# GpSimd's slot-list writes of the attention stage, issued one to a turn

## The chip, the cores and the metric

The kernel runs on one core of a Trainium2 chip. The metric is the device time of one execution in microseconds, the median of several runs.

## What is computed

A layer of self-attention (16 sequences of 256 tokens, 256 features, 16 heads) with a residual and a layer norm is followed by a mixture of 8 experts (two per token, capacity 1280 slots each) with a residual and a layer norm. Cut to what matters here:

```python
gates = softmax(x_flat @ gating_w)                 # x_flat: 4096 tokens after attention and layer norm
topk_w, topk_idx = top_k(gates, 2)
norm_w = topk_w / (sum(topk_w) + 1e-08)
onehot = (flat_e[:, None] == arange(8)[None, :])
position = cumsum(onehot, axis=0) - 1              # the slot of a token's pair in its expert's buffer
valid = position < capacity
buf = zeros((8, capacity, d)).at[flat_e, pos_scatter].set(x_flat[flat_t], mode='drop')
h = maximum(einsum('ecd,edh->ech', buf, w1) + b1, 0)
out_e = einsum('ech,ehd->ecd', h, w2) + b2
out = zeros_like(x_flat).at[flat_t].add(out_e[flat_e, pos] * w_eff)
```

## The kernel before

The attention stage runs over turns, eight to a sequence. Every engine walks the same turns in its own program, and a table of offsets says in which turn a step of sequence m stands: a step with offset 40 of sequence 3 stands in turn 8*3+40. The turns are only an order in which each engine's instructions are written out. No engine waits for a turn; it waits for semaphores alone. So two steps of one engine trade places only if another step stands in a turn between the old and the new one.

For each sequence GpSimd (POOL) does four things in the order of its turns. It splits the transposed x into a high and a low part (L543, L547). It turns the row statistics `mv` into `rstd` and `shift` of the layer norm (L554 to L560), which wait for VectorE's `mv_done`. For the sequences 0 to 11 it works out the slots `dest` and the token and weight `item` (function `entries`, L486 to L524); for the sequences 12 to 15 VectorE does that (`last_entries`, ending in `weight_done` at L869). Then it writes these entries to the slot list in HBM with four indirect DMAs (L533, function `into_lists`): two tiles of 128 tokens, c, and two choices of expert, k. Each DMA writes 128 entries of 8 bytes. `dest` and `item` have four buffers, so sequence m uses number m % 4.

The constant WRITE holds the turns of the writes, one tuple for each step, and in each tuple an offset for the ordinary sequences (0 to 11), one for the sequences 12 and 13, one for 14 and one for 15. The writes of sequence 13 (`FIRST`) are issued in turn 153 instead, after the layer-norm factors of sequence 14.

What hangs on the writes stands at the end of the attention stage. SyncE's queue (SP) loads the list of expert 0 for the first 256 slots as soon as all writes of the sequences 0 to 11 have landed (`list0_loaded`), the next 256 slots when those of sequence 12 have landed too (`list1_loaded`), and behind that the early part of the other experts' lists (L443). GpSimd then gathers the rows of these two chunks with two indirect DMAs each (L1348, `gather(0, 0)` and `gather(0, 1)`, turn 149), and TensorE transposes the gathered rows (L1664). After the writes of the sequences 13, 14 and 15 the late part of the lists is loaded (L454, L455), and the expert stage goes on with the later chunks.

Of the kernel before, what the change touches and what calls it, by code (L numbers as in the profile page):

```python
# [41 lines left out]
def build(nc, x_d, wq_d, wk_d, wv_d, wo_d, gw_d, w1_d, b1_d, w2_d, b2_d, out_d):  # L42
# [40 lines left out]
    with top:  # L83
# [21 lines left out]

        g = locals()
        first = attention(nc, g)
        second = experts(nc, g)
        g["lists"] = second[9]
# [32 lines left out]
def due(turn, offset, count):  # L142


    n, rest = divmod(turn - offset, 8)
    return n if rest == 0 and 0 <= n < count else None
# [11 lines left out]
def pair_of(turn, offset, count):  # L158


    n, u = divmod(turn - offset, 8)
    return (n, u) if 0 <= n < count else None


def attention(nc, g):
    (x_v, x1_v, acc_v, list_v, x1_d, acc_d, list_d) = (
        g["x_v"], g["x1_v"], g["acc_v"], g["list_v"], g["x1_d"], g["acc_d"], g["list_d"])
    NB, S, D, T, R, H = g["NB"], g["S"], g["D"], g["T"], g["R"], g["H"]
    QC, DK, HH, NE, FT, FF, CAP, BLK = g["QC"], g["DK"], g["HH"], g["NE"], g["FT"], g["FF"], g["CAP"], g["BLK"]
    SCALE, TRASH, TOPK = g["SCALE"], g["TRASH"], g["TOPK"]  # L170
# [8 lines left out]
    with ctx:  # L179
        def sem(name):  # L180
            return ctx.enter_context(nc.semaphore(name))

        def sb(name, shape, dt=F32):
            return ctx.enter_context(nc.sbuf_tensor(name, shape, dt))
# [74 lines left out]
        dest = [sb(f"dest{i}", [P, QC, TOPK], I32) for i in range(4)]  # L259
        item = [sb(f"item{i}", [P, QC, TOPK, 2], I32) for i in range(4)]  # L260
# [36 lines left out]
        listed = [sem(f"listed{i}") for i in range(4)]  # L297
# [5 lines left out]
        UT, AT, O, LIST = 34, 36, 38, 50  # L303
        LN, LG, PICK, SEEN, EX = (40, 40, 40, 40), (41, 41, 41, 41), (43, 43, 43, 42), (44, 43, 43, 42), (45, 44, 45, 43)
        X1, STORE, POS, SLOT = (42, 46, 45, 44), (48, 48, 48, 45), (46, 44, 45, 43), (47, 45, 45, 44)
        ENTRY, WRITE = (48, 45, 45, 44), ((51, 46, 46, 45), (52, 47, 50, 46))
        LAST = 8 * (NB - 1) + WRITE[1][3] + 1
        LTAIL = NB - 4
        EARLY, FIRST = g["EARLY"], NB - LATE
        END = 8 * (NB - 1)  # L310
# [13 lines left out]
        def routed(turn, stage):  # L324

            for m in range(NB):
                if turn == 8 * m + stage[0 if m < LTAIL else max(m - NB + 4, 1)]:
                    return m
            return None
# [41 lines left out]
        def sync_program(sp, lists):  # L371
# [14 lines left out]

            for turn in range(LAST + 1):
                n = due(turn, -14, NB)
# [68 lines left out]
        def gpsimd_program(pool, gather):  # L457
# [65 lines left out]
                pool.wait_ge(token_done, m + 1)  # L523
                nc.gpsimd.tensor_scalar(tok[:, :], tok[:, :], float(S), None, ALU.add).then_inc(tok_done, 1)  # L524

            def into_lists(m, c):
                if m == 0 and c == 0:
                    pool.wait_ge(filled, 80)
                pool.wait_ge(dest_done, m + 1)
                pool.wait_ge(token_done, m + 1)  # L530
                pool.wait_ge(weight_done, m + 1)
                for k in range(TOPK):
                    nc.gpsimd.indirect_dma_start(  # L533
                        out=list_d, out_offset=bass.IndirectOffsetOnAxis(ap=dest[m % 4][:, c, k:k + 1], axis=0),
                        in_=item[m % 4][:, c, k, :], in_offset=None, bounds_check=NE * CAP - 1,
                        oob_is_err=False).then_inc(listed[m % 4], 16)

            for turn in range(LAST + 1):
                n = due(turn, XT, NB)
                if n is not None and n >= 2:  # L540
                    pool.wait_ge(xT_copied, n - 1)
                    pool.wait_ge(v_ready, QC * (n - 1))
                    nc.gpsimd.tensor_copy(xT_hi[n % 2][:, :, :], xT_f[:, :, :]).then_inc(xT_hi_done, 1)  # L543
                n = due(turn, XT + 1, NB)
                if n is not None and n >= 2:
                    pool.wait_ge(xT_hi_done, n + 1)
                    nc.gpsimd.tensor_tensor(xT_lo[n % 2][:, :, :], xT_f[:, :, :], xT_hi[n % 2][:, :, :].bitcast(F32),  # L547
                                            ALU.subtract).then_inc(xT_lo_done, 1)
                m = due(turn, LN[0] + 1, NB)
                if m is not None:  # L550
                    pool.wait_ge(mv_done, m + 1)
                    pool.wait_ge(x1_done, m)
                    pool.wait_ge(ex_done, QC * m)
                    nc.gpsimd.tensor_scalar(veps[:, :], mv[:, :, 1], EPS, None, ALU.add).then_inc(norm_parts, 1)  # L554
                    pool.wait_ge(norm_parts, 2 * m + 1)
                    nc.gpsimd.tensor_tensor(rstd[:, :], veps[:, :], expo[:, 0:QC], ALU.pow).then_inc(rstd_done, 1)
                    nc.gpsimd.tensor_scalar(nmean[:, :], mv[:, :, 0], -1.0, None, ALU.mult).then_inc(norm_parts, 1)
                    pool.wait_ge(norm_parts, 2 * m + 2)
                    pool.wait_ge(rstd_done, m + 1)
                    nc.gpsimd.tensor_tensor(shift[:, :], nmean[:, :], rstd[:, :], ALU.mult).then_inc(shift_done, 1)  # L560
                m = due(turn, LIST, LTAIL)
                if m is not None:
                    entries(m)
                for c in range(QC):
                    m = routed(turn, WRITE[c])
                    if m is not None and m != FIRST:
                        into_lists(m, c)
                    if turn == END - 8 + LN[0] + 1:
                        into_lists(FIRST, c)
                if turn == END + PV0 + 4:  # L570
                    pool.wait_ge(v_ready, QC * NB)
                    pool.wait_ge(g["list0_loaded"], 16)
                    gather(0, 0)
                    pool.wait_ge(g["list1_loaded"], 16)
                    gather(0, 1)

        def scalar_program(act, rows_hi, relu):
# [39 lines left out]

            for turn in range(LAST + 1):
                if turn == K + 2:
# [86 lines left out]
        def vector_program(dve, rows_lo, halves):  # L706
# [166 lines left out]

            for turn in range(LAST + 1):
                if turn == K + 2:
# [95 lines left out]
        def tensor_program(pe, transposes, layer1):  # L971
# [95 lines left out]

            for turn in range(LAST + 1):
                p = pair_of(turn, S0, NB)
# [119 lines left out]
            pe.wait_ge(y_done, QC * NB)  # L1189

        return sync_program, gpsimd_program, scalar_program, vector_program, tensor_program


# [602 lines left out]
```

## Time and profile before

| | |
|---|---|
| median of 3 runs | 822.04 us (821.6 to 822.65) |
| span of the profiled execution | 856.8 us |
| TensorE busy | 784.5 us, 92% |
| VectorE busy | 605.1 us, 71% |
| ScalarE busy | 442.1 us, 52% |
| GpSimd busy | 410.2 us, 48% |
| GpSimd slot-list writes (L533) | 64 DMAs, 65.5 us |

The profile shows one execution, and gives its span but no time of its own beside it; the span is 34.8 us longer than the median of the runs. Rows of the timeline give the start and the length of a group of instructions in us, the engine, the line, the operation and its tiles, and in brackets how long the engine sat idle before and what ended that. The turns of the attention stage end at about 380 us; the experts follow.

### The profile page before, as it was taken

The numbers are of one execution on the slowest core, as the hardware profiler recorded it, in microseconds if no ns is written. First come the engines' busy times: TensorE is split into PE (matmuls) and PEld (weight loads), VectorE is DVE, ScalarE is ACT, GpSimd is POOL, SyncE is SP. The second block draws the span as 40 slices with busy tenths as digits, with TensorE's granted clock in tenths as the row PEclk, the third lists the DMA queues.
The fourth block names the chain that finished last, engine by engine and source line by source line (L and its number), as shares of the span: only waits on it lengthen the run. The fifth ranks groups of instructions, "written<-read, shape, count | busy, mean of one in ns | idle before, by whom it ended". The sixth has DMA issues, their size and how long they took to land.

```text
span 856.8 us, 16628 instructions
## 1 busy us (share of the span) xinstructions
PE 784.5 (92%) x5919; PEld 648.5 (76%) x5919; DVE 605.1 (71%) x1325; ACT 442.1 (52%) x753; POOL 410.2 (48%) x595
## 2 busy tenths in 40 slices
PE   7699989999989985896999999999999999999994
PEld 7577766677667653585889898898898888988993
DVE  5768878888888885683756856756657568665983
ACT  3166757777666664542534534534345345443670
POOL 1011245555555546457146445254364462556675
PEclk9799999999999998799899999999999999999998
DMA  5677765555555572326145245253352451533741
GB/s 158 135 165 161 161 153 113 114 113 114 116 114 110 115 141 73 116 51 180 20 91 109 41 89 115 43 130 50 81 111 40 96 112 31 140 57 57 288 179 46
DMA packets 71534, 92.75 MB, mean 108 GB/s; under 512 B 12972, under 2 KB 55885, under 8 KB 71324
## 3 DMA queue, kind: packets, MB, share of 16 engines
q1 hardware_dynamic: 53308, 67.95, 31.0%
q0 software_dynamic: 16928, 22.15, 14.9%
q10 hardware_dynamic: 1216, 1.57, 0.8%
q8 instruction: 48, 0.79, 0.4%
q14 instruction: 34, 0.28, 0.1%
HBM read 39.18 MB, written 26.89 MB: 77 GB/s over the span
## 4 chain that ended last, share of the span: by engine, by line
PE 69%; DVE 14%; issue 5%; POOL 3%; another core or an unknown queue 3%; DMA 2%; ACT 2%; ACTq 1%; POOLq 0%; DVEq 0%; SPq 0%
PE bank L1718 14%; DVE negm L890 10%; PE wide L1687 8%; PE wide L1685 8%; PE wide L1686 8%; PE bank L985 7%; PE bank L1720 7%; PE wide L1030 5%; PE bank L1664 2%; PE wide L1048 2%; PE bank L1095 2%; PE bank L1064 1%; PE bank L994 1%; POOL slot_list L533 1%
## 5 line engine op out<-in xcount | busy, mean ns | idle before, releaser
L1359 POOL DMA_INDIRECT acc_rows<-o_w,lists x70 | 120.4, 1720 | 181.6 <-ACT o_w L1508 167.9
L890 DVE TENSOR_REDUCE negm<-wide 128x4 f32<-128x1024 f32 x128 | 156.1, 1222 | 50.5 <-PE wide L1030 31.7
L630 ACT ACTIVATE probs<-wide 128x1024 f32<-128x1024 f32 x128 | 131.0, 1024 | 89.1 <-PE wide L1048 68.9
L1475 ACT ACTIVATE h<-wide,b1T 128x512 f32<-128x512 f32 (+1 forms) x200 | 115.0, 600 | 96.8 <-PE wide L1687 69.1
L1720 PE MATMUL bank<-stack,h_lo 128*128 128x256 f32 x560 | 156.9, 280 | 0.0
L1685 PE MATMUL wide<-g_hi,stack 128*128 128x512 f32 (+1 forms) x400 | 140.8, 352 | 5.2 <-DVE g_lo L1536 4.1
L1687 PE MATMUL wide<-g_hi,stack 128*128 128x512 f32 (+1 forms) x400 | 140.1, 350 | 0.1
L1686 PE MATMUL wide<-g_lo,stack 128*128 128x512 f32 (+1 forms) x400 | 140.1, 350 | 0.0
L1508 ACT ACTIVATE o_w<-o_b,lists 128x256 f32<-128x256 f32 x70 | 35.7, 510 | 148.6 <-DVE o_b L1646 135.5
L1718 PE MATMUL bank<-stack,h_hi 128*128 128x512 f32 x304 | 108.7, 401 | 1.3 <-DVE o_b L1646 1.3
L1720 PEld LDWEIGHTS bank<-stack,h_lo 128*128 128x128 f32 x560 | 105.6, 189 | 0.0
L1348 POOL DMA_INDIRECT rows<-x_rows,lists x80 | 84.3, 1054 | 29.5 <-issue 23.9
L1718 PE MATMUL bank<-stack 128*128 128x512 f32 x256 | 90.4, 396 | 0.0
L1685 PEld LDWEIGHTS wide<-g_hi,stack 128*128 128x128 f32 x400 | 75.9, 190 | 16.4 <-DVE g_lo L1536 4.4
L1030 PE MATMUL wide<-stack 48*128 48x256 f32 x512 | 65.5, 335 | 24.8 <-DVE negm L890 21.2
L1030 PEld LDWEIGHTS wide<-stack 48*128 48x128 f32 x512 | 40.2, 191 | 62.0 <-DVE negm L890 28.7
L1644 DVE TENSOR_TENSOR low<-bank,b_all 128x256 f32<-128x256 f32 x70 | 29.6, 422 | 81.4 <-PE bank L1720 69.4
L1687 PEld LDWEIGHTS wide<-g_hi,stack 128*128 128x128 f32 x400 | 75.9, 190 | 10.6 <-issue 0.3
L1686 PEld LDWEIGHTS wide<-g_lo,stack 128*128 128x128 f32 x400 | 76.0, 190 | 9.7
L1064 PE MATMUL bank<-probs,v_aug 128*32 128x256 f32 x1024 | 72.4, 402 | 9.3 <-ACT probs L630 9.3
L543 POOL CAST xT_hi<-xT_f 128x512 fp32r<-128x512 f32 x14 | 8.5, 610 | 148.3 <-ACT xT_f L585 148.3
L533 POOL DMA_INDIRECT slot_list<-item,dest x64 | 65.5, 1023 | 25.7 <-issue 23.6
(211 smaller groups left out, 1640.9 us busy)
## 6 DMA issues: line engine op xcount, KB each, us to landing
stack<-qk SPq DMA_DIRECT2D x180, 128.0 KB, 4.2
w_raw<-in_L_ffn_w SPq DMA_DIRECT2D x16, 1024.0 KB
x_sb<-in_L_attn_x SPq DMA_DIRECT2D x16, 256.0 KB, 5.1
x_rows<-x SPq DMA_DIRECT2D x16, 256.0 KB
acc_rows<-x SPq DMA_DIRECT2D x16, 256.0 KB
acc_sb<-acc_rows SPq DMA_DIRECT2D x8, 512.0 KB, 11.1
out<-acc_sb SPq DMA_DIRECT2D x8, 512.0 KB
x_rows<-zrow SPq DMA_DIRECT2D x2, 1152.0 KB, 6.6
```

The source lines that it names most:

```text
L630: nc.scalar.activation(probs[:, i % 4].rearrange("p x c t -> p x (c t)"), shifted_banks(i)[:, :, :], ACT.Exp, scale=SCALE).then_inc(exp_do ...
L890: nc.vector.tensor_reduce(negm[n % 2][:, :, :, u].rearrange("p c x -> p x c"), score_banks(PAIRS * n + u)[:, :, :].rearrange("p x (c t) -> ...
L1030: ins = nc.tensor.matmul(out[:, x, c * S:c * S + S], st[k, u, 0, c * P:c * P + P], st[k, u, 1, :], start=True, stop=True, tile_position=(H ...
L1064: ins = nc.tensor.matmul(out, v_aug[n % VB][:, c, 4 * t + j, :], probs[:, u % 4, j % 2, c, :], start=(c == 0), stop=(c == QC - 1), tile_po ...
L1348: nc.gpsimd.indirect_dma_start(out=rows[c][:, r, :], out_offset=None, in_=x1_d, in_offset=bass.IndirectOffsetOnAxis(ap=lists[:, e, QC * c ...
L1359: nc.gpsimd.indirect_dma_start(out=acc_d, out_offset=bass.IndirectOffsetOnAxis(ap=lists[:, e, QC * c + r, 0:1], axis=0), in_=o_w[c][:, r, ...
L1475: ins = nc.scalar.activation(h[u % 2][:, t], banks[BZ[u % 4]][:, t], ACT.Relu, bias=b1T[:, FT * e + f:FT * e + f + 1])
L1685: nc.tensor.matmul(out, w1_hi[:, k, fs], g_hi[i % 2][:, k, cols], start=(k == 0), stop=False)
L1686: nc.tensor.matmul(out, w1_hi[:, k, fs], g_lo[i % 2][:, k, cols], start=False, stop=False)
L1687: ins = nc.tensor.matmul(out, w1_lo[:, k, fs], g_hi[i % 2][:, k, cols], start=False, stop=(k == DK - 1))
L1718: nc.tensor.matmul(banks[BO[r]], H_hi[:, f, rs], w2_both[:, f, :, :].rearrange("p x d -> p (x d)"), start=(f == 0), stop=False)
L1720: ins = nc.tensor.matmul(out_half(r, 1), H_lo[:, f, rs], w2_hi[:, f, :], start=False, stop=(f == FT - 1))
```

## The change

The table of the writes gets four entries instead of two, one for each DMA, and `into_lists` issues one DMA instead of two. Each call carries the three waits that formerly stood ahead of a pair.

```diff
-        ENTRY, WRITE = (48, 45, 45, 44), ((51, 46, 46, 45), (52, 47, 50, 46))
-        LAST = 8 * (NB - 1) + WRITE[1][3] + 1
+        ENTRY, WRITE = (48, 45, 45, 44), ((52, 46, 46, 45), (53, 47, 46, 45), (54, 48, 50, 46), (55, 49, 50, 46))
+        LAST = 8 * (NB - 1) + WRITE[3][3] + 1
...
-            def into_lists(m, c):
-                if m == 0 and c == 0:
+            def into_lists(m, i):
+                c, k = divmod(i, TOPK)
+                if m == 0 and i == 0:
                     pool.wait_ge(filled, 80)
                 pool.wait_ge(dest_done, m + 1)
                 pool.wait_ge(token_done, m + 1)
                 pool.wait_ge(weight_done, m + 1)
-                for k in range(TOPK):
-                    nc.gpsimd.indirect_dma_start(
-                        out=list_d, out_offset=bass.IndirectOffsetOnAxis(ap=dest[m % 4][:, c, k:k + 1], axis=0),
-                        in_=item[m % 4][:, c, k, :], in_offset=None, bounds_check=NE * CAP - 1,
-                        oob_is_err=False).then_inc(listed[m % 4], 16)
+                nc.gpsimd.indirect_dma_start(
+                    out=list_d, out_offset=bass.IndirectOffsetOnAxis(ap=dest[m % 4][:, c, k:k + 1], axis=0),
+                    in_=item[m % 4][:, c, k, :], in_offset=None, bounds_check=NE * CAP - 1,
+                    oob_is_err=False).then_inc(listed[m % 4], 16)
...
-                for c in range(QC):
-                    m = routed(turn, WRITE[c])
+                for i in range(QC * TOPK):
+                    m = routed(turn, WRITE[i])
                     if m is not None and m != FIRST:
-                        into_lists(m, c)
+                        into_lists(m, i)
                     if turn == END - 8 + LN[0] + 1:
-                        into_lists(FIRST, c)
+                        into_lists(FIRST, i)
```

The four other engines' instructions stand exactly as before. On GpSimd the place of most writes is an ordinary sequence, here the second one: its last step on `tok`, the four writes, and the x split of a later sequence. Before:

```order
L524 TENSOR_SCALAR tok<-tok 128x2 [waits token_done]
L533 DMA slot_list<-item,dest 10240x2 [waits weight_done,token_done,dest_done]
L533 DMA slot_list<-item,dest 10240x2
L533 DMA slot_list<-item,dest 10240x2 [waits weight_done,token_done,dest_done]
L533 DMA slot_list<-item,dest 10240x2
L543 CAST xT_hi<-xT_f 128x512 [waits v_ready,xT_copied]
L547 TENSOR_TENSOR xT_lo<-xT_f,xT_hi 128x512 [waits xT_hi_done]
```

After:

```order
L524 TENSOR_SCALAR tok<-tok 128x2 [waits token_done]
L533 DMA slot_list<-item,dest 10240x2 [waits weight_done,token_done,dest_done] x4
L543 CAST xT_hi<-xT_f 128x512 [waits v_ready,xT_copied]
L547 TENSOR_TENSOR xT_lo<-xT_f,xT_hi 128x512 [waits xT_hi_done]
L554 TENSOR_SCALAR veps<-mv 128x2 [waits ex_done,x1_done,mv_done]
```

No instruction traded places there; the second and the fourth write carry three waits of their own now. The same holds for the writes of the sequences 13, 14 and 15.

The one place where GpSimd's order differs is the end of the attention stage, from the last `tok` of sequence 11 to the first gathers. `item3,dest3` are sequence 11, `item0,dest0` sequence 12, and L554 to L560 are the layer-norm factors of sequence 13. Before:

```order
L524 TENSOR_SCALAR tok<-tok 128x2
L533 DMA slot_list<-item3,dest3 10240x2 x4
L533 DMA slot_list<-item0,dest0 10240x2 x4
L554 TENSOR_SCALAR veps<-mv 128x2
L556 TENSOR_TENSOR rstd<-veps,expo 128x2
L557 TENSOR_SCALAR nmean<-mv 128x2
L560 TENSOR_TENSOR shift<-nmean,rstd 128x2
L1348 DMA rows0<-x1_rows,lists 128x256 x2
L1348 DMA rows1<-x1_rows,lists 128x256 x2
```

After:

```order
L533 DMA slot_list<-item3,dest3 10240x2 x2
L533 DMA slot_list<-item0,dest0 10240x2
L533 DMA slot_list<-item3,dest3 10240x2
L533 DMA slot_list<-item0,dest0 10240x2
L533 DMA slot_list<-item3,dest3 10240x2
L533 DMA slot_list<-item0,dest0 10240x2
L554 TENSOR_SCALAR veps<-mv 128x2
L556 TENSOR_TENSOR rstd<-veps,expo 128x2
L557 TENSOR_SCALAR nmean<-mv 128x2
L560 TENSOR_TENSOR shift<-nmean,rstd 128x2
L533 DMA slot_list<-item0,dest0 10240x2
L1348 DMA rows0<-x1_rows,lists 128x256 x2
```

The writes of the two sequences alternate from the third on, and the last write of sequence 12 moved behind the four small steps of the layer norm of sequence 13, just ahead of the gathers.

## Rows read from the trace of the kernel before

**Rows 1.** The page: the span, and TensorE's granted clock in 40 slices.

```profile
span 856.8 us, 16628 instructions
...
PEclk9799999999999998799899999999999999999998
```

**Rows 2.** Timeline of POOL, writes of an ordinary sequence and what follows them.

```profile
252.78 0.98 POOL L533 DMA_INDIRECT slot_list<-item,dest  x1 [0.30 <-issue]
254.07 0.97 POOL L533 DMA_INDIRECT slot_list<-item,dest  x1 [0.30 <-issue]
255.34 0.97 POOL L533 DMA_INDIRECT slot_list<-item,dest  x1 [0.30 <-issue]
263.06 0.61 POOL L543 CAST xT_hi<-xT_f 128x512 fp32r<-128x512 f32 x1 [6.75 <-ACT xT_f L585]
```

**Rows 3.** Timeline of POOL, the end of the attention stage.

```profile
328.88 0.97 POOL L533 DMA_INDIRECT slot_list<-item,dest  x1 [0.30 <-issue]
...
332.70 0.97 POOL L533 DMA_INDIRECT slot_list<-item,dest  x1 [0.30 <-issue]
...
336.53 0.97 POOL L533 DMA_INDIRECT slot_list<-item,dest  x1 [0.30 <-issue]
341.33 0.22 POOL L554 TENSOR_SCALAR veps<-mv 128x2 f32<-128x2 f32 x1 [3.83 <-DVE mv L939]
...
344.87 1.20 POOL L560 TENSOR_TENSOR shift<-nmean,rstd 128x2 f32<-128x2 f32 x1
346.23 1.10 POOL L1348 DMA_INDIRECT rows<-x_rows,lists  x1 [0.17 <-issue]
...
348.88 0.95 POOL L1348 DMA_INDIRECT rows<-x_rows,lists  x1 [0.30 <-issue]
350.13 0.95 POOL L1348 DMA_INDIRECT rows<-x_rows,lists  x1 [0.30 <-issue]
```

**Rows 4.** Timeline of DVE, one stop in a sequence, and around the last writes.

```profile
257.51 1.23 DVE L890 TENSOR_REDUCE negm<-wide 128x4 f32<-128x1024 f32 x1 [1.34 <-remote]
...
331.60 0.17 DVE L869 TENSOR_TENSOR item<-ex,inv_t 128x4 f32<-128x4 f32 x1
...
342.21 0.67 DVE L956 CAST stack<-w_raw 128x1024 fp32r<-128x1024 f32 x1
...
344.78 1.23 DVE L958 TENSOR_TENSOR stack<-w_raw,stack 128x1024 fp32r<-128x1024 f32 x1
```

**Rows 5.** Timeline of SP's DMA queue, the list loads and what follows.

```profile
342.46 2.02 SPq L440 DMA_DIRECT2D lists<-slot_list  x2
344.53 0.43 SPq L443 DMA_DIRECT2D lists<-slot_list  x1
358.22 0.37 SPq L406 DMA_DIRECT2D x_rows<-x  x1
```

**Rows 6.** DMA issues, KB each and median us from issue to landing.

```profile
lists<-slot_list SPq DMA_DIRECT2D x2, 2.0 KB, 1.7
```

**Rows 7.** The chain that ended last: start, us, and what.

```profile
329.99 9.16 another core or an unknown queue
...
359.81 0.23 POOL veps L554
...
380.63 3.17 DMA slot_list<-item,dest
```

**Rows 8.** Timeline of PE, the transposes of the first gathered rows.

```profile
360.85 0.60 PE L1664 MATMUL bank<-ident,rows 128*128 128x128 f32 x4
...
364.99 0.63 PE L1664 MATMUL bank<-ident,rows 128*128 128x128 f32 x4
```

**Rows 9.** Timeline of POOL, behind the layer norm of sequence 14.

```profile
361.24 0.20 POOL L560 TENSOR_TENSOR shift<-nmean,rstd 128x2 f32<-128x2 f32 x1
...
368.13 0.97 POOL L533 DMA_INDIRECT slot_list<-item,dest  x1 [1.12 <-issue]
...
376.96 1.89 POOL L533 DMA_INDIRECT slot_list<-item,dest  x1 [0.30 <-issue]
```

## The prediction

> **What bounds the kernel now.** I read the page first for the span [rows 1], then the chain of work that ended last. The chain is mostly TensorE, but from 359.81 us to the landing of a list write that starts at 380.63 it goes through GpSimd's queue [rows 7]: there GpSimd's instructions are on the path that sets the end, and a microsecond lost on them is lost in the time. Next I read GpSimd's timeline in three places: an ordinary sequence, where the writes are far from any limit; the end of the attention stage, where the change reorders them; and the stretch on the chain, where it only adds waits. Last, SP's queue and TensorE's transposes say who waits for the reordered writes.
>
> In an ordinary sequence the last write ends at 255.34 + 0.97 = 256.31, and GpSimd then sits idle for 6.75 us until ScalarE's copy of the transposed x is there [rows 2]. Nothing on GpSimd waits behind the writes, and nobody reads the list before the end of the stage.
>
> **The change part by part.** *The turns of the sequences 0 to 10.* Moving the four writes from the turns 51 and 52 to 52 to 55 passes no other GpSimd instruction: the printed order is the same, and an engine doesn't wait for turns. So the writes will stand where they stood, back to back, one each 1.27 us. Cost 0 us. If the idle 6.75 us behind them were gone, a longer run of writes would push the x split of a later sequence; nothing here makes the run longer, though.
>
> *The waits.* 32 of the 64 writes get three waits more, all for semaphores that the write ahead of them has seen already. The rows show both kinds before the change: the write at 254.07 has three waits in front of it, those at 252.78 and 255.34 have none, and all three come 0.30 us behind their predecessor [rows 2]. So a set of satisfied waits between two writes costs 0. A bound from above: GpSimd's 1.12 us in front of the write at 368.13 [rows 9], less the plain 0.30, is 0.82 us, but that one really waited for VectorE. On the chain six writes get such waits (two each of the sequences 13, 14, 15), so the bound is 6 x 0.82 = 4.9 us; I take 0, since the rows at 0.30 are the same case and that one isn't. A gain is excluded, as nothing is taken away.
>
> *The alternation of sequences 11 and 12.* The third write is now the first of sequence 12. It needs VectorE's weights, which are there at 331.60 + 0.17 = 331.77 [rows 4], while GpSimd has finished the second write at 328.88 + 0.97 = 329.85 and would be ready at 330.15 [rows 3]. In the order before, sequence 12 began at 332.70 and waited for nothing. So GpSimd now stands for about 1.7 us and issues its third to seventh write from about 331.9 on, 1.27 us apart; the seventh ends at 331.9 + 4 x 1.27 + 0.97 = 338.0. Before, the eighth ended at 336.53 + 0.97 = 337.50. Behind it stand the layer-norm factors of sequence 13, and they waited for VectorE's `mv` until 341.33, after 3.83 us of idleness [rows 3]. The hole is covered by these 3.83 us; without that cover it would cost 0.5 us. Cost 0.
>
> *The last write of sequence 12.* It now follows the shift of sequence 13, which ends at 344.87 + 1.20 = 346.07 [rows 3]. With a gap of some 0.6 us (an estimate between the 0.30 and the 1.12 of the rows) it starts at about 346.7 and ends at 347.7. The first gather slips from 346.23 to about 348.0. SP may load the second list piece only when this write has landed: 346.7 + 3.17 = 349.9, with the landing time of the write on the chain [rows 7]. It was issued between 342.46 and 344.48 before [rows 5]. It lands 1.7 us later [rows 6], at 351.6, and so the gathers of the second chunk start at about 351.9 instead of 348.88 and end 2.2 us later, at 354.1. Who waits? GpSimd's own next step is the layer norm of sequence 14, at 359.81 [rows 7]: 5.7 us of cover. SP's queue holds the early list of the other experts behind it, which is read only after all attention work, and then the store at 358.22 [rows 5]; SP is free at about 350.8. TensorE transposes the first chunk at 360.85 and the second at 364.99 [rows 8]; with some 2 to 3 us for a gather to land (estimate from the 3.17 and the 1.7 above), the rows are there by about 353 and 357. Cover 8 us each. Cost 0; beyond 5.7 us of further delay it would count on the chain one for one.
>
> The Trainium skill ("SBUF — State Buffer", section "SBUF: two separate sides") has a rule that speaks against the new place: GpSimd can't write the descriptors of its DMAs while VectorE runs a copy that uses both ports. VectorE splits w1 from 342.21 to 346.01 [rows 4], and GpSimd's shift took 1.20 us in that stretch against 0.20 us later [rows 3, 9]; the trace agrees that GpSimd suffers there. By the rows the moved write starts after 346.07, clear of it; by the rule, if it fell into it, it would take something like the 1.89 us of the write at 376.96 [rows 9] instead of 0.97, 0.9 us more, also under the cover. The sum would be 0 by either.
>
> **The sum** is 0 + 0 + 0 + 0. It is made on the profiled execution (span 856.8 us), and I carry differences to the median of 822.04 us one to one. The 34.8 us between them matter for the risk, since the trace holds stops that no semaphore explains. One of 9.16 us, with an unnamed releaser, stands just in the stretch of the reordered writes [rows 7].
>
> **The rivals.** *Slower: the cover is made by that stop.* If the timed executions don't have the 9.16 us, the layer norm of sequence 14 is due at 350.65. TensorE's clock is 0.7 of full on average in slice 16, 342.7 to 364.1 us [rows 1], after the stop; had it stayed high, the 17.1 us from 342.7 to 359.8 could be 12.0, and the step due at 345.5. GpSimd then runs without idling: factors of sequence 13 from 338.1 to 339.7 (1.63 us, as 359.81 to 361.44 [rows 7, 9]), the moved write at 340.3, landing at 343.5, the list at 345.2, the second gathers over at 347.7. They would keep the layer norm of sequence 14 waiting 2.2 us; 0.8 us of that is given back where GpSimd waits for VectorE's entries of sequence 14 anyway (1.12 against 0.30 [rows 9]). That is +1.4 us, 823.4. The order before has its second gathers over at about 344, so pays nothing. It passes 0.2% (1.64 us, about what a measurement of this kernel tells from no change) when that step is due before 345.2, and reaches +2.8 us at 343.6. For it: the gap of 34.8 us. Against it: I can't see which of these stops a timed run has, and every step must shrink by the full amount.
>
> *Faster: the unbroken run of writes is itself what stops the others.* ScalarE resumes at 329.99 + 9.16 = 339.15, 1.65 us after the eighth write has ended; in the ordinary sequence VectorE resumes at 257.51 after a stop of 1.34 us, 1.20 us after the fourth write [rows 2, 4]. If eight unbroken writes make 9.16 us and four make 1.34, a run broken by the 1.7 us hole into two and five would make about 3.3 us by interpolation: up to 5.9 us less in the trace, a time near 816 to 821, say 819. Against it: no engine but GpSimd waits for the issue of a write.
>
> *The change does something in ordinary sequences after all*, by its waits: bound +4.9 us above, and any value of 0.27 us a write or more on the chain would pass 0.2%. Nothing but that one far row speaks for it.
>
> **How the numbers follow.** No effect beyond 0.5 us: 0.60. The covered gathers become visible: 0.24, somewhat more than half of it above 0.2%. A shorter stop: 0.11. The waits cost something, or code fetched at other moments: 0.05, mostly small or up. So faster 0.12, same 0.66, slower 0.22. The time is that of the first case, with a trifle for the runs' own spread: 822.2 us; its own range is 821.4 to 823.2. The range for 8 in 10 reaches into the slower rival to +2.6 us (824.6) and into the faster one to -1.4 us (820.6).
>
> **What would show it.** In the changed kernel's timeline of GpSimd: four writes of an ordinary sequence still 1.27 us apart with 0.30 us between all of them, and the idle time behind them near 6.7 us; a hole of about 1.7 us before the third of the last run; the moved write near 346.7, a list load by SP near 350, the second gathers near 352, and the layer norm of sequence 14 still ended by VectorE's `mv`, near 359.8. The forecast is wrong if that last step is ended by a gather instead, if the gap between writes grows, or if the stop of 9.16 us changes its length.

## The result, and the profile after

The change made the kernel slower. Its median is 824.72 us in six runs (823.86 to 826.41) against 821.82 us for the kernel before in six runs beside it; the ratio is 1.0047, with a 95% interval of 1.0037 to 1.0058, which is 3.0 to 4.8 us, 3.9 us in the middle. The ratios in this document are not quotients of two medians; these two medians alone lie 2.9 us apart. The forecast was 822.2 us with a range up to 824.6.

The page of the changed kernel has a span of 822.6 us, 34.2 us less than the one that the prediction was read from, and TensorE's clock doesn't dip in the slices of the stretch:

```profile
span 822.6 us, 16660 instructions
...
PEclk9689999999999999999999999999999999999998
...
PE 77%; DVE 13%; issue 4%; POOL 3%; DMA 2%; ACTq 1%; ACT 0%; POOLq 0%; DVEq 0%; SPq 0%
```

The stops with unnamed releasers are gone from it, too. So the two pages can't be laid side by side, and I took a second profile of the kernel before (the first experiment below). This is GpSimd's timeline there, with a span of 817.7 us, at the place that answers to [rows 3]:

```profile
308.88 1.12 POOL L533 DMA_INDIRECT slot_list<-item,dest  x1 [0.55 <-issue]
310.30 0.98 POOL L533 DMA_INDIRECT slot_list<-item,dest  x1 [0.30 <-issue]
...
315.00 0.97 POOL L533 DMA_INDIRECT slot_list<-item,dest  x1 [1.17 <-DVE item L869]
...
318.91 0.97 POOL L533 DMA_INDIRECT slot_list<-item,dest  x1 [0.30 <-issue]
319.95 1.02 POOL L554 TENSOR_SCALAR veps<-mv 128x2 f32<-128x2 f32 x1
322.20 0.23 POOL L560 TENSOR_TENSOR shift<-nmean,rstd 128x2 f32<-128x2 f32 x1
...
325.59 0.95 POOL L1348 DMA_INDIRECT rows<-x_rows,lists  x1 [0.30 <-issue]
326.84 0.95 POOL L1348 DMA_INDIRECT rows<-x_rows,lists  x1 [0.31 <-issue]
328.81 0.22 POOL L554 TENSOR_SCALAR veps<-mv 128x2 f32<-128x2 f32 x1 [1.02 <-DVE mv L939]
...
336.72 0.97 POOL L533 DMA_INDIRECT slot_list<-item,dest  x1 [0.71 <-issue]
...
341.56 1.16 POOL L533 DMA_INDIRECT slot_list<-item,dest  x1 [0.90 <-issue]
...
349.41 0.97 POOL L533 DMA_INDIRECT slot_list<-item,dest  x1 [0.30 <-issue]
```

And this is the same stretch of the changed kernel:

```profile
311.48 1.12 POOL L533 DMA_INDIRECT slot_list<-item,dest  x1 [0.55 <-issue]
312.90 0.97 POOL L533 DMA_INDIRECT slot_list<-item,dest  x1 [0.30 <-issue]
316.56 0.97 POOL L533 DMA_INDIRECT slot_list<-item,dest  x1 [2.69 <-DVE item L869]
...
321.74 1.55 POOL L533 DMA_INDIRECT slot_list<-item,dest  x1 [0.30 <-issue]
323.37 0.22 POOL L554 TENSOR_SCALAR veps<-mv 128x2 f32<-128x2 f32 x1
...
325.61 1.09 POOL L533 DMA_INDIRECT slot_list<-item,dest  x1 [0.60 <-issue]
327.07 1.01 POOL L1348 DMA_INDIRECT rows<-x_rows,lists  x1 [0.37 <-issue]
328.38 0.95 POOL L1348 DMA_INDIRECT rows<-x_rows,lists  x1 [0.30 <-issue]
332.20 0.94 POOL L1348 DMA_INDIRECT rows<-x_rows,lists  x1 [2.87 <-DMA lists<-slot_list]
333.45 0.95 POOL L1348 DMA_INDIRECT rows<-x_rows,lists  x1 [0.30 <-issue]
334.47 0.23 POOL L554 TENSOR_SCALAR veps<-mv 128x2 f32<-128x2 f32 x1
...
341.99 0.97 POOL L533 DMA_INDIRECT slot_list<-item,dest  x1 [0.30 <-issue]
...
346.56 1.08 POOL L533 DMA_INDIRECT slot_list<-item,dest  x1 [0.60 <-issue]
...
354.32 0.97 POOL L533 DMA_INDIRECT slot_list<-item,dest  x1 [0.30 <-issue]
```

The stretch begins anywhere from 308.88 to 312.53 us, depending on the profile. In the changed kernel the 2.6 us of difference are there long before the first list write, which starts at 110.89 us: the last step of the first layer norm's factors stands at 86.00 us, against 83.39 in the second profile of before. So times are counted from here on from the first write of sequence 11 (308.88 and 311.48 us here); "+20" is 20 us after it. The reader is to see three things. A hole of 2.69 us stands before the third write. GpSimd stands 2.87 us before the third gather (332.20), and a DMA ended that wait: the list load. And the layer norm of sequence 14, which before came 1.02 us after GpSimd had fallen idle, now follows the gathers at once: it starts at +22.99 instead of +19.93, 3.06 us later, though VectorE's `mv` was ready earlier (at +19.06; in the profile before at +19.84). The last list write starts at +42.84 instead of +40.53, and from the first write of sequence 11 to the end the span is 511.1 us instead of 508.8. That is 2.3 us, against 2.9 between the medians and 3.9 by the ratio; two single profiles don't give more.

SP's queue shows the list loads. In the changed kernel, with the start of each group (L440 are the two pieces of expert 0's list, 5.63 us from the start of the first to the end of the second):

```profile
322.71 5.63 SPq L440 DMA_DIRECT2D lists<-slot_list  x2
328.39 0.43 SPq L443 DMA_DIRECT2D lists<-slot_list  x1
329.17 0.37 SPq L406 DMA_DIRECT2D x_rows<-x  x1
329.58 1.23 SPq L407 DMA_DIRECT2D acc_rows<-x  x1
330.86 0.47 SPq L446 DMA_DIRECT2D b_all<-in_L_ffn_b  x1
```

The second piece is issued at 322.71 + 5.63 - 0.33 = 328.01 us, and the view of DMA issues has it landing 3.9 us later:

```profile
lists<-slot_list SPq DMA_DIRECT2D x1, 2.0 KB, 3.9
```

### The profile page after: what moved, and what is told of

Same layout as the page of the kernel before. It is cut to its first block, busy times and chain, and to the rows that moved or that the text cites. A ratio compares the mean times of both kernels' runs of the same rounds, so it can differ in the third digit from the quotient of the medians.

```text
span 822.6 us, 16660 instructions
## 1 busy us (share of the span) xinstructions
PE 773.8 (94%) x5919; PEld 644.5 (78%) x5919; DVE 604.2 (73%) x1325; ACT 442.8 (54%) x753; POOL 408.3 (50%) x595
## 4 chain that ended last, share of the span: by engine, by line
PE 77%; DVE 13%; issue 4%; POOL 3%; DMA 2%; ACTq 1%; ACT 0%; POOLq 0%; DVEq 0%; SPq 0%
PE bank L1718 15%; PE bank L985 12%; DVE negm L890 9%; PE wide L1685 9%; PE wide L1687 9%; PE wide L1686 9%; PE bank L1720 8%; PE wide L1030 7%; PE bank L1664 2%; PE wide L1048 2%; PE bank L994 2%; PE bank L1095 1%; POOL slot_list L533 1%; POOL out L1415 1%; DMA rows<-x_rows,lists 1%
## 5 line engine op out<-in xcount | busy, mean ns | idle before, releaser
L1064 PE MATMUL bank<-probs,v_aug 128*32 128x256 f32 x1024 | 68.5, 385 | 1.0 <-ACT probs L630 1.0
```

## The experiments

Each ratio is to the kernel before, timed on the same chip; 0.1% is 0.8 us.

**The kernel before once more**, unchanged, one profile.

> The kernel before, unchanged, for a second profile: the one shown has stops with unnamed releasers (one of 9.16 us) and a span of 856.8 us, the profile of the change has a span of 822.6 us and none of them. Theory A (the moved write holds up the second list piece, and the gathers that wait for it hold up the layer norm of sequence 14 on GpSimd): the span is near 820 us, the layer norm of sequence 14 starts when VectorE's mv is there, near 330.6 us, and the second gathers end before it, near 328.5. Theory B (the order of the writes doesn't matter; something else in the program, as the added waits, costs the time): GpSimd's layer norm of sequence 14 starts as late as in the change, near 334.5.

The span was 817.7 us, and the layer norm of sequence 14 started 1.02 us after the second gathers were over, ended by VectorE's `mv`: theory A's picture. Its start at 328.81 is not far from the 330.6 expected, but the whole stretch stood 2.6 us earlier. More important is what isn't there. The view of waits of the first profile of before has these rows:

```profile
ACT probs L630 <- remote: 17.1, 4, 9.2
DVE negm L890 <- remote: 15.3, 10, 3.1
DVE y L761 <- remote: 7.5, 1, 7.5
```

No profile of the twelve other executions (this one, the changed kernel and the ten kernels below) has a wait on "remote". The stops belonged to that one profiled execution.

**The waits alone.**

```diff
-        ENTRY, WRITE = (48, 45, 45, 44), ((52, 46, 46, 45), (53, 47, 46, 45), (54, 48, 50, 46), (55, 49, 50, 46))
+        ENTRY, WRITE = (48, 45, 45, 44), ((51, 46, 46, 45), (51, 46, 46, 45), (52, 47, 50, 46), (52, 47, 50, 46))
```

(All diffs here are against the changed kernel.)

> The waits alone: four calls with three waits each, but the turns of before, so that no instruction of GpSimd trades places. Theory A: no change, within 0.1% of before (0 to 0.5 us). Theory B (the added waits cost the time): all of it, +2.9 to +3.9 us.

Ratio 1.0002, 0.9991 to 1.0013. Theory B, which wanted at least 2.9 us, falls, and the prediction's 0 for the waits stands within an interval that still allows 1.1 us. This kernel has the same 16660 instructions in its profile as the changed one, so the length of the program isn't what costs either. From the first write of sequence 11 the profile took 508.7 us to the end, as before.

**The alternation alone.**

```diff
-(55, 49, 50, 46))
+(55, 48, 50, 46))
```

> The alternation alone: the writes of the sequences 11 and 12 alternate as in the change, but the last one of sequence 12 stays ahead of the layer norm of sequence 13. Theory A (the moved write is what costs): by the trace of the change the last write would stand at about 323.6 us instead of 325.6, its list piece would be there at 328.5, the second gathers over at 331.3, and the layer norm of sequence 14 starts near 331.4 instead of 330.6: +0.7 us. Theory C (the hole in front of the third write, 2.69 us, and the later layer norm of sequence 13 are what costs): nearly all, +2.5 us or more.

Ratio 1.0027, 1.0014 to 1.0040, or 2.2 us: three times what theory A gave it, and a little under the 2.5 us of theory C, which the interval includes. GpSimd's queue itself does what theory A said: the hole is there (2.69 us), and the layer norm of sequence 14 starts at +20.47, 0.54 us later than before. Something else is late, too, as the timeline of PE shows in the transposes of the gathered rows (the second row of each kernel is the one that counts; [rows 8] are those of before):

```profile
330.85 0.60 PE L1664 MATMUL bank<-ident,rows 128*128 128x128 f32 x4
337.05 0.66 PE L1664 MATMUL bank<-ident,rows 128*128 128x128 f32 x4 [1.80 <-DMA rows<-x_rows,lists]
```

The second gather of that chunk was issued at 329.89 us and its rows were waited for until 337.05. In the second profile of before the same gather was issued at 326.84, ahead of SP's load of the biases (1 MB, L446, 328.55), and TensorE didn't wait. Here it was issued after the load (329.45). Behind TensorE's wait came the `mv` of sequence 15 (+30.24, before +28.80), VectorE's entries of sequence 15 (+34.85, before +33.30), and GpSimd's first write of them:

```profile
346.16 1.12 POOL L533 DMA_INDIRECT slot_list<-item,dest  x1 [0.79 <-DVE item L869]
```

But this reached the end only in small part. In the second profile of before that write starts at +35.58, here at +35.72; the last write starts at +40.81 against +40.53. The first gather of the later chunks starts at +46.95 against +45.75, and most of these 1.2 us arose in the load of the late list (L454), which landed 2.7 us after its issue here and 1.5 us there. So TensorE's wait is seen, but that it makes up the rest of the 2.2 us is not shown.

**The moved write alone.**

```diff
-((52, 46, 46, 45), (53, 47, 46, 45), (54, 48, 50, 46), (55, 49, 50, 46))
+((51, 46, 46, 45), (51, 47, 46, 45), (52, 48, 50, 46), (52, 49, 50, 46))
```

> The moved write alone: sequence 11's four writes, three of sequence 12, the layer norm of sequence 13, and then the last write of sequence 12, without any alternation. Theory A (the moved write is what costs): most of the loss, +1.5 us at least and up to +2.9, with GpSimd idle before the second gathers until the list load has landed, and the layer norm of sequence 14 right behind them. Theory C (the hole): nearly nothing, under 0.5 us, since no hole is left.

Ratio 1.0028, 1.0014 to 1.0041, or 2.3 us, within what theory A gave; theory C, which gave under 0.5 us, falls. There is no hole in GpSimd's writes, and yet GpSimd stands before the second gathers, and the layer norm of sequence 14 is 1.89 us late (+21.82):

```profile
323.75 1.09 POOL L533 DMA_INDIRECT slot_list<-item,dest  x1 [0.60 <-issue]
...
330.37 0.95 POOL L1348 DMA_INDIRECT rows<-x_rows,lists  x1 [2.97 <-DMA lists<-slot_list]
...
332.64 0.22 POOL L554 TENSOR_SCALAR veps<-mv 128x2 f32<-128x2 f32 x1
```

Either half costs about half of the whole or a little more. Their sum of 4.5 us and the 3.9 us of the whole can't be told apart with such intervals.

**The change with the second gathers behind the layer norm of sequence 14.**

```diff
+                if turn == END - 8 + LN[0] + 1:
+                    pool.wait_ge(g["list1_loaded"], 16); gather(0, 1)
                 for i in range(QC * TOPK):
...
                     gather(0, 0)
-                    pool.wait_ge(g["list1_loaded"], 16)
-                    gather(0, 1)
```

> The change, with the two gathers of the second chunk moved behind the layer norm of sequence 14 on GpSimd (ahead of sequence 13's writes), so that no layer-norm step waits behind them. Theory A (GpSimd stands in front of these gathers until the second list piece is there, and everything behind them is late by that): GpSimd's wait of 2.87 us is filled with the 1.6 us of layer norm; sequence 13's writes and all that follows start some 1.6 us earlier than in the change, counted from the first write of sequence 11; the time is 1.0 to 1.6 us under the change's, about 0.3% over before. Theory D (what costs is TensorE's wait for the gathered rows, since the gathers are issued behind the 1 MB bias load): no gain or a small loss, since the gathers are issued no earlier; 0.45 to 0.5% over before.

Ratio 1.0023, 1.0012 to 1.0034, against the change's 1.0037 to 1.0058: the intervals don't touch, and 1.9 us are back of some 3.9, a little more than theory A gave. The layer norm no longer stands behind the list load:

```profile
331.09 0.22 POOL L554 TENSOR_SCALAR veps<-mv 128x2 f32<-128x2 f32 x1 [1.27 <-DVE mv L939]
...
333.21 1.10 POOL L1348 DMA_INDIRECT rows<-x_rows,lists  x1 [0.45 <-issue]
```

The first write of sequence 13 starts at +23.85 instead of +25.26, and TensorE still waits 1.98 us for the rows. What is left of the loss is therefore not the layer norm's place in the queue. Part of it is the queue all the same: the two gathers now stand between the layer norm and the writes with no idle time, so the first write of sequence 13 is still 1.66 us later than before (+22.19).

**The change with the bias load later.**

```diff
-                if turn == END + PV0 + 7:
+                if turn == END + STORE[3] + 1:
                     sp.wait_ge(pv_ready, QUADS * NB)
```

> The change, with SP's load of the biases b2 (1 MB) moved from turn 152 to turn 166, behind the store of sequence 15. Theory A (GpSimd's queue is the path): the gathered rows of the second chunk land earlier and TensorE's 1.47 us of waiting shrinks, but GpSimd's queue stays as it is from the layer norm of sequence 14 on: no gain over the change, or at most 0.3 us. Theory D (the rows' way through the bias load is what costs): 1 to 1.5 us under the change.

Ratio 1.0049, 1.0036 to 1.0062: no gain, as theory A said; theory D falls for the change. TensorE's wait did vanish (the second transposes start at 335.76 with no idle time, though the gathers were issued at 331.72), so the bias load was what delayed the rows. But GpSimd's queue was the later of the two paths: its layer norm of sequence 15 followed at +32.55, when `mv` had been ready since +28.09.

**The alternation alone with the bias load later**, the same edit on the second experiment's kernel.

> The alternation alone (last write of sequence 12 ahead of the layer norm), and the bias load moved to turn 166 as well. In the alternation alone the second gathers were issued at 328.64 and 329.89 us, around the bias load's issue at 329.45, and TensorE stood 1.80 us for their rows; GpSimd then waited 0.79 us for VectorE's entries of sequence 15. Theory D for this kernel (the rows land late because of the bias load, and TensorE's wait delays the last entries): most of the 0.27% goes, 0.7 to 1.8 us under the alternation alone. Theory C (the hole of 2.69 us delays GpSimd's queue itself): it stays at 0.2 to 0.3% over before.

Ratio 1.0019, 1.0009 to 1.0028. The trace did what theory D said: no wait of TensorE, VectorE's entries of sequence 15 at +33.06 instead of +34.85, and the last write at +39.45 instead of +40.81. The first gather of the later chunks came only 0.76 us earlier, at +46.19. The time went down by 0.7 us if by anything; its interval overlaps with that of the alternation alone, so this stays a reading of the trace that the times don't contradict.

**The change with both moved.**

> The change with both: the second gathers behind the layer norm of sequence 14, and the bias load in turn 166. Theory A and D together (GpSimd's queue and TensorE's wait are both late by the same list piece): GpSimd's queue gains 1.6 us as with the gathers moved alone, and TensorE no longer limits, 1.5 to 2.5 us under the change, 0.15 to 0.3% over before. Theory A alone: the same as with the gathers moved alone.

Ratio 1.0032, 1.0023 to 1.0041. That is not better than the gathers moved alone, and the expectation that both gains would add wasn't met. GpSimd's queue kept its gain (first write of sequence 13 at +23.65), but TensorE waited for the late gathers still, 0.88 us.

**The change with the early lists of the other experts loaded later.**

```diff
-                    early = g["early_v"]
-                    sp.dma_start(lists[:, 1:, 0:EARLY // P].rearrange("p e j w -> p e (j w)"), early[:, 1:]).then_inc(g["lists_loaded"], 16)
+                early = g["early_v"]
+                if turn == END + STORE[3] + 1: sp.dma_start(lists[:, 1:, 0:EARLY // P].rearrange("p e j w -> p e (j w)"), early[:, 1:]).then_inc(g["lists_loaded"], 16)
```

> The change, with SP's load of the other experts' early lists (28 KB in 8-byte entries, issued right behind the second list piece) moved to turn 166. In the change the second list piece was issued at 328.01 us and there at 331.9, 3.9 us, where the prediction took 1.7. Theory E (the piece is slowed by that load behind it): it lands 1.5 to 2 us sooner, GpSimd's wait before the second gathers of 2.87 us shrinks to about 1, and the time is 1 to 2 us under the change's. Theory F (the 3.9 us is what such a load takes in this stretch): nothing changes, within 0.5 us of the change, 0.4 to 0.5% over before.

Ratio 1.0038, 1.0024 to 1.0051. GpSimd's wait shrank from 2.87 to 2.16 us, less than theory E wanted, and TensorE's wait for the rows grew to 2.66 us. The time lies between the two theories and its interval overlaps with the change's: not settled.

**A larger dose**: the last write of sequence 12 behind the first chunk's gathers.

```diff
-(55, 49, 50, 46))
+(55, 99, 50, 46))
...
-                    gather(0, 0)
+                    gather(0, 0); into_lists(FIRST - 1, 3)
```

> A larger dose of the same: the change, with the last write of sequence 12 moved one step further, behind the two gathers of the first chunk. The write starts about 2.6 us later (two gathers of 1.3 us). Theory A (the time follows the moment at which the second list piece is there, through GpSimd's queue): the second gathers and the layer norm of sequence 14 come 1.3 to 2.6 us later than in the change, and the time is 1.3 to 2.6 us above it, 0.65 to 0.8% over before. Theory B (the loss is a fixed cost of the reordered program, not of this wait): 0.47% over before, as in the change.

Ratio 1.0073, 1.0051 to 1.0095, or 6.0 us, so 2.1 us above the change, within theory A's 1.3 to 2.6; theory B's 1.0047 lies below the interval, though the two kernels' intervals overlap a little. GpSimd's wait grew:

```profile
335.37 0.98 POOL L1348 DMA_INDIRECT rows<-x_rows,lists  x1 [4.96 <-DMA lists<-slot_list]
...
337.67 0.22 POOL L554 TENSOR_SCALAR veps<-mv 128x2 f32<-128x2 f32 x1
```

The layer norm of sequence 14 starts at +27.17, and from the first write of sequence 11 to the end it takes 515.1 us. Both are 4 us more than in the change, where theory A wanted 1.3 to 2.6; the times show about half of that. TensorE's wait for the second rows grew as well, from 1.47 to 4.61 us, so this dose acts on both paths and by itself doesn't tell them apart.

**A version meant to be faster than before**: the old order, with sequence 13's first write in the idle time ahead of the layer norm of sequence 14, and sequence 14's second write behind the layer norm of sequence 15.

```diff
+        ENTRY, WRITE = (48, 45, 45, 44), ((51, 46, 46, 45), (51, 46, 50, 45), (52, 47, 50, 46), (52, 47, 50, 46))
...
-                    if turn == END - 8 + LN[0] + 1:
+                    if i and turn == END - 8 + LN[0] + 1:
...
-                    gather(0, 1)
+                    gather(0, 1); into_lists(FIRST, 0)
```

> A version meant to beat before: the order of before, but the first write of sequence 13 stands ahead of the layer norm of sequence 14, in the 1.02 us that GpSimd idled there in the second profile of before, and the second write of sequence 14 stands behind the layer norm of sequence 15. Theory A (GpSimd's queue from there on is the path): one write of 1.27 us less in front of the last writes, at a cost of 0.3 us for the layer norm: 0.5 to 1 us under before, which this measurement can hardly tell from nothing. Theory D (TensorE's waits and VectorE's entries of sequence 15 set the last writes): no gain, within 0.1% of before.

Ratio 1.0002, 0.9990 to 1.0013: nothing. In the trace the last write came at +38.67 instead of +40.53, but the rows of the later chunks were gathered only 0.8 us earlier (+44.92 for +45.75). Nothing here beats the kernel before.

**Where the lateness reaches the end.** In all twelve profiles without the long stop, the span ends 462.8 to 463.6 us after the first gather of the later chunks. So what happens behind that gather differs by 0.8 us at most, and these columns (us after the first write of sequence 11) show how lateness gets there:

| kernel | first write of sequence 13 | last write | first later gather | ratio |
|---|---|---|---|---|
| before | 22.19 | 40.53 | 45.75 | 1 |
| write ahead | moved (18.35) | 38.67 | 44.92 | 1.0002 |
| waits alone | 22.17 | 39.51 | 45.66 | 1.0002 |
| alternation, bias load later | 22.51 | 39.45 | 46.19 | 1.0019 |
| alternation alone | 22.73 | 40.81 | 46.95 | 1.0027 |
| both moved | 23.65 | 41.21 | 47.29 | 1.0032 |
| gathers behind the layer norm | 23.85 | 40.81 | 46.73 | 1.0023 |
| moved write alone | 24.08 | 41.64 | 46.36 | 1.0028 |
| early lists later | 24.48 | 42.54 | 48.81 | 1.0038 |
| bias load later | 24.95 | 42.56 | 48.62 | 1.0049 |
| the change | 25.26 | 42.84 | 48.07 | 1.0047 |
| larger dose | 29.44 | 46.98 | 52.10 | 1.0073 |

The first write of sequence 13 says how late GpSimd's queue is, and it orders the kernels nearly as the times do. The last write is a poorer mark: with the waits alone it started 1.02 us earlier than before, and the gather came at the same time.

## Why the prediction was wrong

**The ordinary sequences and the waits.** Right. The order was the same, the writes stayed 1.27 us apart with 0.30 us between them, and the waits alone measured 1.0002. The idle time behind the writes was 5.4 us instead of 6.7, still far from any limit.

**The alternation.** The hole was forecast as 1.7 us and was 2.69. The forecast that it costs 0 rested on 3.83 us of idle time before the layer norm of sequence 13 [rows 3]. In the second profile of before that cover is not there: the factors follow the eighth write directly (318.91 + 0.97, then 319.95), although VectorE's `mv` was ready at +7.08 and the factors began at +11.07. Some of the loss came back in a way that I hadn't counted: before, these factors ran beside VectorE's split of w1 and took from 319.95 to 322.43, 2.48 us, and in the changed kernel, pushed behind the split, 1.64 us. Still the alternation alone cost 2.2 us. That its term was not 0 is shown; in the trace GpSimd's queue is only 0.54 us late by it, and by what the rest comes is open.

**The last write of sequence 12: the step that failed.** It said "GpSimd's own next step is the layer norm of sequence 14, at 359.81 [rows 7]: 5.7 us of cover". In executions without the long stop the cover was the 1.02 us of idle time before that layer norm. The delay was mis-sized as well: the second gathers end 4.0 us later (+22.92 for +18.91), not 2.2, mainly since the load of the second list piece took 3.9 us where 1.7 was taken from [rows 6]. 4.0 less 1.0 is the 3.06 us by which the layer norm is late. TensorE's cover of 8 us was also of that one execution: here it waited 0.90 us for the rows of the first chunk and 1.47 us for those of the second.

**The slower rival was the mechanism**, given a chance of 0.24 and a price of 1.4 to 2.8 us. Its reason was the right one, that the cover was made by the 9.16 us stop [rows 7]. Its sum was short. It counted 2.2 us of lateness for the layer norm where there were 3.06, and took 0.8 us off for a wait of GpSimd that it would fill. The second profile of before had nearly that to give: 0.41 us ahead of sequence 14's first write (a gap of 0.71 for 0.30) and 0.30 behind the layer norm of sequence 15 (0.90 for 0.60). 3.06 less 0.71 is the 2.3 us by which the last write, the later gathers and the end are late in the trace.

Three experiments show together that GpSimd's wait carries the larger part of the loss. The moved write alone brings the wait back and costs 2.3 us. The gathers moved behind the layer norm give 1.9 us back, though TensorE's wait grew from 1.47 to 1.98 us. The bias load moved away takes TensorE's wait for the second rows off and gives nothing back. The larger dose (2.1 us more) agrees. That the rows are late on TensorE because of the bias load is shown in the trace by moving the load; what it costs in time is not measured apart.

**The faster rival** tied the stop to the length of the unbroken run of writes. The second profile of before has the same eight writes, only a gap of 1.17 us in them, and no stop at all. The version with the write ahead has them without any gap (9.17 us from the first to the start of the eighth) and no stop either. It falls.

**The rule on VectorE's copies** (the Trainium skill, "SBUF — State Buffer", section "SBUF: two separate sides") was weighed for the moved write, which did start clear of the split, 325.61 us against the split's end at 322.4. It mattered at two places that I didn't weigh. The seventh write, at 321.74, stood beside the split's last step and took 1.55 us instead of 0.97, in agreement with the rule. And the layer norm's factors, which no longer ran beside the split, took 0.84 us less.

What stays open: how the alternation alone costs 2.2 us; the 0.6 us between the 2.3 us of the two profiles and the medians' 2.9, or 1.6 us to the ratio's 3.9; and what made the stops in the first profile. A part of the second may go with TensorE's clock. The mean granted clock of the changed kernel's six runs was 0.983, that of the 80 runs of the kernel before beside the experiments 0.985, and among those 80 runs 0.01 of clock goes with 3.5 us, which makes some 0.7 us (an estimate). Whether that is a cause of the longer time or follows from it, no run here shows.

## What to carry to other kernels

A cover that is read from one profile is only as good as that execution: when the span is 34.8 us above the runs' median and waits on unnamed releasers stand in the stretch, take them out before counting slack, and take that case as the forecast. In an order that is written by turns, first look which instructions really trade places; a small edit to a table acted here at one spot, the end of the stage, where a write that another engine's load waits for moved behind four small steps. An instruction that waits in GpSimd's in-order queue is priced by what stands behind it, so a write that releases such a wait belongs as early as it can be issued: moved behind four small steps it cost 2.3 us here. And when profiles of one kernel differ, look for a late instruction from which the rest takes the same time in all of them, here the first later gather; what is late by then is the loss.

## What the runs showed of the hardware

Three semaphore waits that are already satisfied, put before each of 32 indirect DMAs on GpSimd, cost nothing that could be measured (1.0002, 0.9991 to 1.0013), and the gap between two such DMAs stayed at 0.30 us. The same 2 KB load from HBM took 1.6 us from issue to landing in the first profile of before, 2.4 us in the second and 3.9 us in the changed kernel, where no DMA packet moved in the 0.3 us around its issue (327.9 to 328.2); gathers of the first chunk, two stores of 256 KB and the 1 MB load of the biases were issued while it was under way. Gathered rows were usable 7 us after their gather when it was issued just behind a 1 MB load (329.89 to 337.05 us, and TensorE had stood 1.80 us for them); with that load moved away TensorE didn't wait (a gather at 332.97, transposes at 335.76, in the change with the bias load later). And the four small factors of a layer norm on GpSimd took 2.48 us where their first step fell beside VectorE's split (1.02 us for 0.22) and 1.64 us behind it.
